# Edge pass of a four-layer graph network: one product of 150 columns for each pair of destination columns, weights completed on VectorE, and a ring of five PSUM banks

## What is computed

```
h = jnp.maximum(_layernorm(x, axis=-1), 0.0)
x = x + _L0_gnn_ref(h, edge_attr_32, ..., edge_index)
h = jnp.maximum(_layernorm(x, axis=-1), 0.0)
x = x + _L1_gnn_ref(h, edge_index, ...)
...
msg_input = jnp.concatenate([x[src], x[dst], edge_attr], axis=-1)
h = jax.nn.relu(msg_input @ W1.T + b1)
messages = h @ W2.T + b2
agg = jax.ops.segment_sum(messages, dst, num_segments=x.shape[0])
...
msg = h[src] * norm[:, None]
out = jax.ops.segment_sum(msg, dst, num_segments=n)
```

## Time and profile before

| | us |
|---|---|
| median of 3 runs | 2386.38 (2385.16 to 2386.99) |
| profiled execution, its time | 2400.12 |
| profiled execution, its span | 2398.6 |
| PE busy | 1557.9 (65%) |
| DVE busy | 957.5 (40%) |
| POOL busy | 900.3 (38%) |
| ACT busy | 659.2 (27%) |
| mean DMA rate over the span | 103 GB/s |

### The profile page before, as it was taken

How to read it: one execution, slowest core, us unless ns; L and a number is a source line. 1 busy time by engine, 2 the same in 40 slices (tenths; PEclk the granted TensorE clock), 3 DMA queues, 4 the chain that set the end, 5 groups by cost and what they waited for, 6 DMA issues and landing times. The chain is left out here.

```text
span 2398.6 us, 31354 instructions
## 1 busy us (share of the span) xinstructions
PE 1557.9 (65%) x10942; PEld 1012.2 (42%) x10942; DVE 957.5 (40%) x2738; ACT 659.2 (27%) x1639; POOL 900.3 (38%) x911
## 2 busy tenths in 40 slices
PE   1405555555555555555455553998978989599997
PEld 1303333434333333334333342675645556445544
DVE  5644454545445454545455446221322124301111
ACT  1303333333333333334333311121323332100000
POOL 5046666666666666666666622000000000000001
PEclk8655666665556666666666655998889989799999
DMA  6423434343443434343343432000100001594571
GB/s 160 119 62 101 119 104 124 109 125 106 112 119 103 124 109 125 107 121 109 106 123 107 121 111 59 1 1 8 41 15 2 5 9 33 191 332 174 200 270 60
DMA packets 203234, 247.43 MB, mean 103 GB/s; under 512 B 36541, under 2 KB 177416, under 8 KB 203061
## 3 DMA queue, kind: packets, MB, share of 16 engines
q1 hardware_dynamic: 174260, 184.35, 24.3%
q0 software_dynamic: 28800, 60.80, 9.7%
HBM read 174.04 MB, written 57.60 MB: 97 GB/s over the span
## 5 line engine op out<-in xcount | busy, mean ns | idle before, releaser
L809 POOL DMA_INDIRECT arena<-dram_PHL,src_of x806 | 823.8, 1022 | 495.0 <-issue 213.2
L1026 PE MATMUL psum<-arena 128*128 128x100 f16 x1568 | 220.9, 247 | 260.0 <-issue 215.0
L1026 PEld LDWEIGHTS psum<-arena 128*128 128x128 f16 x1568 | 174.7, 129 | 392.5 <-issue 370.5
L1010 PE MATMUL psum<-arena 128*128 128x128 f16 x1612 | 209.0, 288 | 180.7 <-issue 146.5
L961 ACT ACTIVATE arena<-psum 128x512 f16<-128x512 f32 x202 | 120.5, 596 | 649.5 <-remote 574.2
L1028 PE MATMUL psum<-arena 128*128 128x50 f16 x1568 | 213.3, 229 | 57.0 <-issue 56.5
L1010 PEld LDWEIGHTS psum<-arena 128*128 128x128 f16 x1612 | 147.6, 130 | 216.4 <-issue 215.8
L2275 POOL DMA_DIRECT2D parts_a<-dram_x x7 | 5.3, 763 | 609.1 <-POOLq L2473 586.0
L880 DVE SCALAR_TENSOR_TENSOR agg_all<-psum,agg_all 128x64 f32<-128x64 f32 x202 | 44.5, 221 | 403.2 <-remote 399.4
L1028 PEld LDWEIGHTS psum<-arena 128*128 128x128 f16 x1568 | 171.5, 114 | 71.1 <-issue 69.8
L869 DVE SCALAR_TENSOR_TENSOR arena<-psum,arena 128x512 f16<-128x512 f32 x202 | 138.4, 685 | 151.7 <-issue 103.8
(11 more groups left out here) (359 smaller groups left out, 2135.3 us busy)
## 6 DMA issues: line engine op xcount, KB each, us to landing
arena<-dram_aw SPq DMA_DIRECT2D x7, 6400.0 KB, 20.4
dram_aw<-arena SPq DMA_DIRECT2D x196, 200.0 KB
arena<-dram_aw SPq DMA_DIRECT2D x3, 4800.0 KB, 17.1
arena<-in_ea_quads SPq DMA_DIRECT2D x51, 256.0 KB
arena<-dram_rel SPq DMA_DIRECT2D x51, 256.0 KB
arena<-arena SPq DMA_DIRECT2D x408, 32.0 KB
arena<-dram_PHL,src_of POOLq DMA_INDIRECT x806
arena<-dram_aw SPq DMA_DIRECT2D x2, 4000.0 KB, 14.8
```

Of the source, the lines that this page charges most:

```text
L809: nc.gpsimd.indirect_dma_start(gathered_p[:, slot, k, :], None, d["PHL"], bass.IndirectOffsetOnAxis(ap=src_of[:, b:b + 1], axis=0)).then_i ...
L1010: nc.tensor.matmul(out[:, k * P:(k + 1) * P], side[:, s, at:at + P], node_side[:, g % NAB, part * D:(part + 1) * D], start=(part == 0 and ...
L1026: nc.tensor.matmul(out, hot_lo[:, u, p, :], hot_key[:, u, p, 0:2].rearrange("p a k -> p (a k)"), start=True, stop=False)
```

## The change

- `multiply` makes one product of 150 columns for a pair, where it made one of 100 and one of 50. Counts, high weight parts and low weight parts stand apart in PSUM.
- The 8 pairs of a column block are taken in three units of 3, 3 and 2 pairs (`UNIT`, `UNITS`). A unit fills one PSUM bank: three thirds of 150 (or 100) columns. The units go through a ring of five banks (`RING`), and each is released by itself.
- `matrix_out` takes each unit out by itself: three ACT instructions for a unit, nine for a column block, where there were three.
- The low weight part is added by DVE where it leaves PSUM (`whole_weights`), three instructions for a column block; the store now waits for DVE (`weights_out`).
- To free banks, `build` has one bank instead of two (`NPRE` = 1), and `sum_up` one instead of two, so `sum_up(g)` waits for `add(g - 1)`.
- ACT's order within a step is turned: `matrix_out(s-1)` stands ahead of `relu(s)`.

```diff
-    NS, NPRE, NPG, NAB = 3, 2, 6, 8
+    NS, NPRE, NPG, NAB = 3, 1, 6, 8
...
-        def pair_of(r, p):
-            return psum[:, 2 + 2 * (r % 2) + p // 4, (p % 4) * P:(p % 4) * P + 2 * PKEY]
+        def pairs_of(j):
+            return range(j * UNIT, min((j + 1) * UNIT, PAIRS))
+
+        def bank_of(r, j):
+            return psum[:, 1 + (UNITS * r + j) % RING, 0:len(pairs_of(j)) * 3 * PKEY]
+
+        def third_of(r, j, q):
+            n = len(pairs_of(j)) * PKEY
+            return bank_of(r, j)[:, q * n:(q + 1) * n].rearrange("p (a t) -> p t a", t=NT)
...
         def agg_of(g):
-            return psum[:, 6 + g % 2, 0:BAND]
+            return psum[:, 6, 0:BAND]
...
                 def store_weights(r):
-                    sp.wait_ge(adj_out, r + 1)
+                    sp.wait_ge(weights_out, UNITS * (r + 1))
...
                     if r >= 2:
-                        dve.wait_ge(multiplied, r - 1)
+                        dve.wait_ge(multiplied, UNITS * (r - 1))
...
+                def whole_weights(r):
+                    whole = aw_out[:, r % 3, :].rearrange("p (t n) -> p t n", t=NT)
+                    for j in range(UNITS):
+                        dve.wait_ge(halves_out, UNITS * r + j + 1)
+                        nc.vector.scalar_tensor_tensor(out=columns_of_unit(whole, j), in0=third_of(r, j, 2),
+                                                       scalar=1 / UP, in1=columns_of_unit(whole, j), op0=ALU.mult,
+                                                       op1=ALU.add).then_inc(weights_out, 1)
...
                         pair_hots(s + 1)
+                    if 1 <= s <= J:
+                        whole_weights(s - 1)
                     if s < MG:
                         low_parts(s)
...
                 def matrix_out(r):
-                    act.wait_ge(multiplied, r + 1)
                     if r >= 3:
                         act.wait_ge(aw_stored[r % 3], 16 * (r // 3))
...
+                    for j in range(UNITS):
+                        unit = UNITS * r + j
+                        act.wait_ge(multiplied, unit + 1)
+                        nc.scalar.activation(columns_of_unit(flat_adj[:, :, r * W:(r + 1) * W], j), third_of(r, j, 0),
+                                             ACT.Copy, saturate=True)
...
                 for s in range(MG + 1):
+                    if 1 <= s <= J:
+                        matrix_out(s - 1)
                     if s < MG:
                         relu(s)
-                    if 1 <= s <= J:
-                        matrix_out(s - 1)
...
                 def multiply(r):
                     u = r % 2
                     pe.wait_ge(hot_keys, r + 1)
-                    if r >= 2:
-                        pe.wait_ge(adj_out, r - 1)
-                    for p in range(PAIRS):
-                        out = pair_of(r, p)
-                        nc.tensor.matmul(out, hot_lo[:, u, p, :], hot_key[:, u, p, 0:2].rearrange("p a k -> p (a k)"),
-                                         start=True, stop=False)
-                        done = nc.tensor.matmul(out[:, PKEY:2 * PKEY], hot_lo[:, u, p, :], hot_key[:, u, p, 2],
-                                                start=False, stop=True)
-                    done.then_inc(multiplied, 1)
+                    for j in range(UNITS):
+                        unit = UNITS * r + j
+                        if unit >= RING:
+                            pe.wait_ge(weights_out, unit - RING + 1)
+                        for i, p in enumerate(pairs_of(j)):
+                            thirds = bank_of(r, j).rearrange("p (q x) -> p q x", q=3)
+                            done = nc.tensor.matmul(thirds[:, :, i * PKEY:(i + 1) * PKEY], hot_lo[:, u, p, :],
+                                                    hot_key[:, u, p], start=True, stop=True)
+                        done.then_inc(multiplied, 1)
...
-                    if g >= 2:
-                        pe.wait_ge(added, g - 1)
+                    if g:
+                        pe.wait_ge(added, g)
```

More of the change, by code:

```diff
@@ L50 @@
 PKEY = PAIR * NT
+UNIT = 3
+UNITS = -(-PAIRS // UNIT)
+RING = 5
 PCOLS = -(-(J * PAIRS + 1) // P)
@@ L694, in edge_pass @@
         ea_sq = sb("ea_sq", [P, QUADS], F32)
-        over = sb("count_over", [P, J], F32)
-        over_of = sb("over_of", [P, NKEY], F16)
+        over = sb("count_over", [P, UNITS * J], F32)
+        over_of = sb("over_of", [P, UNIT * PKEY], F16)
         last = sb("flag_parts", [P, 8], F32)
@@ L963, in matrix_out @@
                 def matrix_out(r):
[L964 removed]
                     if r >= 3:
                         act.wait_ge(aw_stored[r % 3], 16 * (r // 3))
[L967 to L975 removed]
+                    for j in range(UNITS):
[3 more added lines that the diff above has]
+                                             ACT.Copy, saturate=True)
+                        if unit:
+                            act.wait_ge(counted, unit)
+                        n = len(pairs_of(j))
+                        nc.scalar.activation(over_of[:, 0:n * PKEY].rearrange("p (t a) -> p t a", t=NT),
+                                             third_of(r, j, 0), ACT.Relu, bias=minus_most[:, 0:1],
+                                             accum_out=over[:, unit:unit + 1]).then_inc(counted, 1)
+                        nc.scalar.activation(columns_of_unit(
+                            aw_out[:, r % 3, :].rearrange("p (t n) -> p t n", t=NT), j), third_of(r, j, 1), ACT.Copy,
+                            scale=1 / UP).then_inc(halves_out, 1)
                 act.wait_ge(w_in, 32)
```

21 lines of the change are left out of this document (6 added, 15 removed).

## The result

| | before | after |
|---|---|---|
| median, us | 2385.91 (2385.16 to 2386.99, 4 runs) | 2556.93 (2555.39 to 2560.25, 4 runs) |
| ratio, 95% interval | | 1.072 [1.070, 1.074] |
| profiled execution, its span | 2398.6 | 2554.0 |
| PE busy | 1557.9 | 1519.9 |
| DVE busy | 957.5 | 1096.1 |

The changed kernel is 171 us slower, where 32 us of gain were forecast. The two profiled executions are 155 us apart, since the one of the kernel before took 14 us more than its median. All of these 155 us lie in the edge pass: the last relu of the pass starts at 1391.8 us before and at 1548.9 us after, 157 us later.

What follows compares the result with a forecast made beforehand. Late matmul completions on PE were taken to starve POOL in the edge pass. Per four groups 11.4 + 12.2 + 0.25 = 23.9 us for 24.55; 49 quads give 32 us, 2386.4 - 32 = 2354 us; range 2275 to 2460.

Steps and rivals of the forecast that it cites:

- The stops of POOL after two groups: Edge pass: POOL pauses after every eight gathers, 2.06 and 1.81 us, about 4.0 us of waiting per four groups (a quad).
- the late store: Weight store queued on SP behind `load_edges`, which waits for `hots`; `matrix_out` waited 3.22 us, starting 6.16 us after `hots`.
- the 10.4 us from `hots` to the relu: Kernel before: from `hots` of a quad's last group (900.80) to the first relu after the stall (911.24).
- counted by number, 3.0 per us: PE: matmul completions limited by their number, not columns; 32 fewer in a quad, 10.7 us less.
- The first leg: From a quad's last `hots` through `matrix_out`, relu, cut and `build` to the relu after the stall: 11.4 us.
- the second leg: From the relu after the stall to the next quad's last `hots`: 68 completions, 12.2 us, plus 0.25 for the add.
- The curve: Measured matmul completions after a POOL pause: 34 at 3.3 us, 58 at 8.9, 3.0 per us from there.
- The ring itself: `multiply`'s third unit waits for DVE's first unit of block g - 1, so for the store; no cost added, DVE path 21.8 us.
- matrix_out ahead of the relu: Rival: nothing saved on completions, relu after the store 1.0 to 1.9 us later per quad; 2435 to 2479 us, chance 0.28.
- The 28.2 us a quad, 2565 us: Case where each group waits for its own POOL pause, 20.6 + 4 x 1.9 us; left outside the range.
- POOL as the bound: Rival: completions keep up, so a quad is POOL's 20.6 us; 2190 us, halfway 2290; chance 0.10 for 2190 to 2310.
- The output in three runs: Rival: `multiply` products writing three runs of 50 columns take 0.25 us for 0.12; 2447 us, chance 0.05.

Runs made afterwards that it cites:

- the run with a busy POOL: Kernel before with plain loads in place of the gathers and a memset on POOL after each load: 2084.41 us; kernel before on the same chip 2211.71.

## Why the prediction was wrong

**The waits of before were read rightly, the completions were not.** The stops of POOL after two groups, the late store and the 10.4 us from `hots` to the relu are there. But the completions were misread in the rows themselves. `build(119)`, 10 matmuls, stands behind the sum that was added at 911.13, and its relu starts at 911.24: the last 10 of the 34 completions since 903.14 came within 0.11 us, and so they did not come at 3.0 per us. The same quad has matmuls 0.7 to 1.4 us apart from 918.64 on, and the first 25 us of the pass up to 2.8 us apart under unbroken gathers, from which "counted by number, 3.0 per us" would not have been taken.

**The first leg was right.** Forecast 11.4 us from `hots` to the relu after the stall; measured 10.9, with `matrix_out` 5.3 us after `hots` (6.16 forecast) and 5.6 for the rest (5.3 summed). So the two errors cancel in part.

**The step that failed is the second leg**: "completions ... I count them by number", 68 of them in 12.2 us. Measured: 26 in 6.2 us (relu to relu), 26 in 3.9, the last 16 up to the add in 5.75, 15.85 in all. The curve had been read in a quad in which POOL's stops and PE's work coincided. In the changed kernel they don't: PE stands for 8.58 us until 1023.43, waiting for DVE's unit, and of the 4.16 us up to 1027.94 in which POOL stops, another 1.51 us waiting for DVE; what it does in that stop is the last two products, one sum and one build. So the ring uses up the time in which PE could run fast, and its other work falls under the gathers. That is my reading of the timeline; no run tests it by itself, and since PE follows POOL's stops only after 1.5 us and more, its limits are soft. It fits that the stores moved take the cost away (2412 us beside 2404), and that the change costs 6 us where the gathers do not hold PE back. That the step fails is shown without it: 8 matmuls fewer a step in the kernel before gave 0.2 us a quad of 10.7, and 8 more in the changed kernel cost nothing. 10.9 + 16.1 = 27.0 us for this quad; 23.9 had been forecast.

**The ring itself was seen and priced at nothing.** "The third unit of `multiply(g)` waits for DVE's first unit of block g - 1, so it too hangs on the late store", and "DVE alone would be there sooner", at 21.8 us. Measured with plain loads: 20.5 us, so the size was about right. But with plain loads the kernel before takes 17.4. The sum compared this 21.8 only with the leg that ends last, and did not ask what becomes of the slack between 17.4 and 24.6 us when 3 us of it are spent.

**The rival that came nearest** is matrix_out ahead of the relu, 2435 to 2479. Its mechanism is part of it (50 us together with the single bank), its size too small, since it took the ring as open at PE. The 28.2 us a quad, 2565 us, that were left outside the range are within 0.4 us of the mean quad. That is chance if the reading above holds: not that each group waits for a stop, but that stop and work fall apart.

**The other rivals.** POOL as the bound: not on the occasion of the result, but on the later ones the kernel before is bound by it, at 20.9 us. The output in three runs costs nothing. The changed kernel's PE timeline at the start of the pass:

```profile
160.12 1.21 PE L1052 MATMUL psum<-arena 128*128 128x150 f16 x8
```

Eight products in 1.21 us, with one of 0.31 us at the end, are 0.13 us apart, as the pairs were before. The Trainium skill's page "PSUM — Partial Sum Buffer" (Specifications) has any non-contiguous pattern slow matmuls significantly; this row speaks against it for runs of 50 fp32 columns. The Trainium skill's page "TensorE: Matmul & The Clock Gate" (Back-to-back issue gap) gives for isolated matmuls at the lower clock columns over clock, an estimate of 0.125 us for 150 columns, with which the row agrees; the verdict that it implied, no gain on PE, held.

**ACT and DVE.** A `whole_weights` instruction took 0.290 us on average (0.26 to 0.31 forecast). ACT's instructions were dearer than summed on average, since several were drawn out in time: L989 0.359, L994 0.453, L997 0.368 us in the changed kernel, and with the stores first 0.296 for L987. Neither decides anything here.

## What to carry to other kernels

A wait that costs nothing is priced by the slack over it. Before an edit ties more work to a late transfer, write down the ring that this closes (store, output buffer, PSUM bank, product, load, store) and its length beside the next longest one: here 20.5 us against 17.4, and under a bound of 20.9 it was free, under a bound made of stops and slow stretches it cost 3.1 us a quad.

Order on a shared DMA queue is part of such a ring. The loads of `load_edges` moved behind the stores on SP took the change's cost from 171 to 8 us, and gave the kernel before no more than 5.

When an engine is "late" with nothing recorded between, look for a stretch in which the suspected neighbour runs unbroken, and for one in which it is idle, before a rate is taken from a mixture.

## What the hardware showed that was not expected

- On the occasions where the kernel before takes 2385 to 2404 us, matmuls start 0.7 to 2.8 us apart when indirect gathers have run one behind the other for some us, and go on so for 1.5 to 4.5 us after the last one. Without gathers, or with plain DMAs of the same size and number on the same queue, this is gone: 2389 us become 2011 and 2025.
- The same kernel took 2212 us on two other occasions (19 runs at 2201.52 to 2217.78 on one of them), with gathers of the same length (1.009 us for 1.022) and without the slow matmuls. What differs there I can't say, nor whether it is the chip. Every comparison of this kernel depends on which of the two it met: the change is 7.2% slower on the one and 0.35% on the other.
- How a gather holds PE back stays open. Plain loads in place of gathers free it, but they also halve the time that POOL is busy for each (0.54 us for 1.02) and read neighbouring rows, so the indirect form is not shown to be the cause; the run with a busy POOL met the other kind of occasion.
- Where PE is held back, the trace has far fewer records of semaphore updates: about 4,400 between 200 and 1000 us in the kernel before, 20,800 in the same kernel where it took 2212 us, 27,400 with plain loads. That would explain the many releasers called "remote"; whether the missing records and the slow matmuls have one cause was not tried.
- No version that computes all was faster than the kernel before by more than single runs can tell. Where PE is not held back, the 16 gathers of a quad are the bound; where it is, the time that went without them was 377 us.
